# Two small matrix products of a fused transformer kernel as quadrant tiles, with a new interleaving of its first stretch

## The chip, the cores and the metric

The kernel runs as one program on one core of a Trainium2 chip. The metric is the device time of one launch in microseconds. The engines are TensorE (PE, with its weight loads PEld), VectorE (DVE), ScalarE (ACT), GpSimd (POOL) and SyncE (SP); DMAs are issued by SP, ACT and POOL and moved by the core's 16 DMA engines.

## What is computed

A block of six layers over 2048 tokens of width 256 (32 batches of 64), in float32:

```python
x = x + _L0_xattn_ref(_layernorm(x), ctx_768, mask, ...)   # 8 heads of 64 over 256 context rows
x = x + _L0_attn_ref(_layernorm(x), ...)                   # 16 heads of 16, keys and values through a latent
x = x + _L0_ffn_ref(...)                                   # ternary weights
x = x + _L1_xattn_ref(...)                                 # 16 heads of 16
x = x + _L1_attn_ref(...)                                  # gated, squared relu
x = x + _L1_ffn_ref(...)                                   # 160 experts, top 8
```

The change lies in the second layer:

```python
q = (x @ wq.T).reshape(b, s, NH, HD).transpose(0, 2, 1, 3)
k = (x @ wk_a.T @ wk_b.T).reshape(b, s, NH, HD).transpose(0, 2, 1, 3)
v = (x @ wv_a.T @ wv_b.T).reshape(b, s, NH, HD).transpose(0, 2, 1, 3)
```

`x @ wk_a.T` and `x @ wv_a.T` are 64 wide each (the latents); `@ wk_b.T` and `@ wv_b.T` bring them back to 256. These last two are the latent key and value products.

## The kernel before

The 2048 tokens are 16 tiles of 128 (`TILES`), two batches in a tile. The program has three stretches: `phase1` (layers one and two and the norm of the third, all tiles), `phase2` (layers three to five and the routing) and `experts` (layer six). A barrier of all engines stands behind `phase1`. The change is in `phase1`.

Each engine works through its instructions in the order in which they were written, and waits on semaphores at the instructions that need another engine's result. That order comes from `weave`: every part of a tile's work (`keys`, `queries`, `attend`, `unit` 0 to 3, `latent`, `half` 0 and 1, `project`, and so on) is a generator whose `yield` gives the due time of the piece that follows; tile i's parts start at i times a period; and `weave` always writes the piece that is due first. The due times are only an order: nothing waits for them on the chip.

What the prediction's steps touch, with the lines of the profile:

- `keys` (L1261): SP loads the context tile (L1265); for tile 1 it also fetches the weight group "o" (rope table, rotation inputs, `head` and others, L1232), for tile 2 the 31 weights of the later stretches, `loads` (L1277), each adding 16 to `s_load`. PE multiplies by the key weights: L1288 (128 rows) and L1293 (the other 64 rows).
- `keys_out` (L1296): ACT copies the four key banks out, L1302. `queries` (L1328): statistics L1254 to L1256, PE transposes L1361, `xT` L1366, product L1373, ACT copies `qT` out, L1378.
- `attend` (L1417): 16 score products of 64x64 tiles, L1429, in two groups of eight; the first needs `qT` and key copies 0 and 1, the second copies 2 and 3.
- `unit` (L1380): DVE masks and takes the maxima (L1385, L1388), ACT exponentiates (L1396), PE transposes (L1409), DVE or ACT copies out (L1415). `values` L1312, L1317; `gather` L1447 and on.
- `latent` (L1478): PE transposes (L1494), latent product L1508 and queries L1512, ACT copies `lat` (L1516); then the key product L1520 and the value product L1525, both from the 64-row halves of `lat`; DVE copies `qTB` (L1531) and `vx` (L1544), ACT `kx` (L1536). `half` (L1548): score products L1558 (its second group needs `vx`), maxima, exponentials L1572, transposes L1582. `project` (L1589): L1607, L1612, L1627.
- `clearing` (L1644): ACT issues 16 DMAs of 1768 KB that clear the routing table (L1649). `rotate` (L1651): DVE turns the query and key weights by the rope table in three pieces of six operations (L1661 to L1667); the first waits for group "o". `prepare` (L1670): DVE and PE wait until all 31 `loads` have landed (`s_load`), then DVE reduces and scales a few of them (L1674 to L1703).

```python
period = 34.25
parts = [(467.91, keys_values(0, banks_free)), (110.00, clearing()), (41.72, rotate()), (37.04, prepare())]
```

Of the kernel before, what the change touches and what calls it, by code (L numbers as in the profile page):

```python
# [15 lines left out]
P = 128  # L16
# [24 lines left out]
NEG = -3.4028234663852886e38  # L41

# [117 lines left out]
def weave(parts):  # L160

    due = []
    for start, part in parts:
        due.append([start + next(part), len(due), start, part])
    while due:
        due.sort()
        first = due[0]
        at = next(first[3], None)
        if at is None:
            due.remove(first)  # L170
        else:
            first[0] = max(first[0], first[2] + at)


def later_keys(nc, a, G, D, bank, cT, kT, vv, weights, s_ctx):

    pe, act, sp = nc.tensor, nc.scalar, nc.sync
    wka, wkb, wva, wvb, bkd = weights

    def keys_values(i, banks_free=None):  # L180
        z = i % 2
        yield 5.96
        G.wait(sp, "v3", i - 2)
        sp.dma_start(cT[z][:, :, :], a["ctx2"][i]).then_inc(s_ctx[z], 16)
        yield 144.95
# [6 lines left out]
        yield 157.65  # L192
# [3 lines left out]
        for m in range(2):  # L196
            yield (168.53, 169.89)[m]
# [3 lines left out]
        yield 168.10  # L201
        for m in range(2):
            D.wait(pe, f"e{6 + m}", i - 1)
        for t in range(2):
            yield (173.60, 175.54)[t]
            cols = slice(t * DIM, (t + 1) * DIM)
            for m in range(2):
                q = 2 * m + t
# [4 lines left out]
        for m in range(2):  # L213
            yield (180.74, 182.84)[m]
# [7 lines left out]
def phase2(nc, a, turns, keys_values, routes, rings, sem, bank, X, XN, ident, small, dchain, pool_waits, resident, kT, vv, qs, qb, bg2, sc):  # L222
# [5 lines left out]
    with ph:  # L228
# [104 lines left out]
        def stage_c(i):  # L333
            z = i % 2
            yield 131.54
# [5 lines left out]
            yield 135.57  # L341
# [3 lines left out]
            yield 142.54  # L345
# [4 lines left out]
            yield 143.99  # L350
# [6 lines left out]
            yield 145.18  # L357
            C.wait(pool, "var", i)
            C.done(i, "pool", power(stC), "rstd")
            yield 146.27  # L360
# [3 lines left out]
            yield 150.06  # L364
# [3 lines left out]
            yield 149.36  # L368
# [4 lines left out]
            yield 155.21  # L373
# [3 lines left out]
            yield 155.72  # L377
# [7 lines left out]
            yield 160.29  # L385
# [8 lines left out]
        def scores(i, m):  # L394
            z = i % 2
            yield (155.05, 168.93)[m]
# [13 lines left out]
        def softmax(i, u):  # L410
            m, hp, bk = u // 4, u % 4, bank[4 + u % 2]
            yield (161.78, 161.28, 161.07, 163.97, 168.75, 169.00, 192.86, 170.02)[u]
# [3 lines left out]
            yield (163.54, 163.20, 162.31, 166.80, 175.29, 179.64, 199.05, 188.63)[u]  # L416
# [7 lines left out]
            yield (187.67, 162.00, 194.66, 169.27, 200.15, 189.54, 205.24, 196.98)[u]  # L424
# [11 lines left out]
            yield (196.45, 168.22, 195.16, 182.33, 203.51, 197.43, 207.47, 203.11)[u]  # L436
# [5 lines left out]
        def mix(i):  # L442
            z = i % 2
            for m in range(2):
                yield (167.68, 198.02)[m]
# [3 lines left out]
                yield (182.00, 201.83)[m]  # L449
# [7 lines left out]
            yield 204.98  # L457
# [6 lines left out]
            yield 210.31  # L464
            D.wait(pe, "pT6e", i)
            D.wait(pe, "pT7e", i)
# [10 lines left out]
            yield 210.32  # L477
# [3 lines left out]
            yield 210.82  # L481
# [9 lines left out]
            yield 210.82  # L491
# [6 lines left out]
        def stage_e(j):  # L498
            z = j % 2
            yield 196.97  # L500
# [7 lines left out]
            yield 201.92  # L508
            E.wait(pool, "vara", j)
            E.done(j, "pool", power(stE), "rstda")  # L510
            yield 212.05
# [3 lines left out]
            yield 222.30  # L515
# [4 lines left out]
            yield 226.39  # L520
            E.wait(pool, "x5", j - 1)
            E.done(j, "pool", pool.tensor_tensor(xbE[:, :], x4[:, :], bout[:, :], ALU.add), "xbE")
            yield 223.12
# [5 lines left out]
            yield 225.83  # L529
# [3 lines left out]
            yield 233.13  # L533
# [5 lines left out]
            yield 233.39  # L539
# [3 lines left out]
            yield 235.02  # L543
# [4 lines left out]
            yield 234.13  # L548
# [6 lines left out]
            yield 234.92  # L555
# [3 lines left out]
            yield 241.28  # L559
# [6 lines left out]
            yield 235.46  # L566
# [3 lines left out]
            yield 240.77  # L570
# [3 lines left out]
            yield 240.93  # L574
# [3 lines left out]
            yield 241.90  # L578
# [7 lines left out]
            yield 243.21  # L586
# [8 lines left out]
            yield 245.33  # L595
# [5 lines left out]
            yield 244.64  # L601
# [7 lines left out]
            yield 247.42  # L609
# [4 lines left out]
            yield 249.36  # L614
# [5 lines left out]
            yield 249.89  # L620
            E.wait(pool, "varf", j)
            E.done(j, "pool", power(stE), "rstdf")
            yield 252.75
# [8 lines left out]
            yield 253.88  # L632
# [14 lines left out]
        def stage_f(j):  # L647
            z = j % 2
            yield 238.29
# [5 lines left out]
            yield 236.18  # L655
# [3 lines left out]
            yield 239.29  # L659
# [4 lines left out]
            yield 241.15  # L664
# [3 lines left out]
            yield 244.18  # L668
# [3 lines left out]
            yield 244.18  # L672
# [7 lines left out]
            yield 246.99  # L680
# [3 lines left out]
            yield 248.84  # L684
# [6 lines left out]
            yield 248.84  # L691
            R.wait(pe, "before", j)
            R.done(j, "pe", pe.matmul(after, ones[:, 0, :], before[z][:, :], start=True, stop=True), "rank")
            yield 270.19
# [12 lines left out]
            yield 272.07  # L707
# [7 lines left out]
            yield 279.76  # L715
# [3 lines left out]
            for k in range(TOPK):  # L719
                yield (280.87, 280.87, 281.74, 285.93, 290.87, 307.02, 329.57, 324.60)[k]  # L720
# [6 lines left out]
        def count_pages(j):  # L727
            yield 273.00
# [10 lines left out]
        def order_pages():  # L739
# [3 lines left out]
            yield -30.00  # L743
            D.wait(sp, "norm", TILES - 1)
            sp.dma_start(numbers, bc(a["c_pages"], 0, P)).then_inc(s_ids, 16)
            yield 1.00
# [3 lines left out]
            yield 1.50  # L750
# [5 lines left out]
            yield 3.50  # L756
# [95 lines left out]
        for i in range(TILES):  # L852
            parts += [(i * period + 24.00, scores(i, m)) for m in range(2)] + [(i * period + 24.00, softmax(i, u)) for u in range(8)]
            if i:
                parts.append((i * period, keys_values(i)))
# [981 lines left out]
```

## Time and profile before

| | us |
|---|---|
| median of 3 runs | 1413.94 |
| lowest and highest | 1410.7, 1417.48 |
| span of the profiled execution, first to last instruction | 1412.0 |
| own time of the profiled execution | not listed apart from its span |
| of it: `phase1` with its weights' loading | about 486 |
| `phase2` | about 540 |
| `experts` | the rest |

The profile's rows give for an instruction or a run of equal ones the start, the time, the engine, the line, the operation, what it writes and reads, its shape and how often. A float32 matmul leaves two records (x4 is two matmuls), a transpose one. Times that stand behind "PE" are modelled at their end: the distance from one start to the next is the safer measure. Matmuls run on parts of the array at once where their rows and columns of it differ; such a group's records overlap.

### The profile page before, as it was taken

How to read it: one execution, taken by the hardware profiler on the slowest of the kernel's cores; microseconds unless marked ns; L12 is line 12 of the kernel's file. 1: busy time of each engine (PE TensorE's matmuls, PEld its weight loads, DVE VectorE, ACT ScalarE, POOL GpSimd, SP SyncE). 2: the span in 40 equal slices, each digit the busy share in tenths (PEclk: the TensorE clock that was granted, in tenths of full speed). 3: DMA queues.
4: the chain of work that ended last, by engine and by line, in shares of the span. 5: the costliest groups of instructions: out<-in, count | busy, mean ns of one | idle time of the engine just before them, and what ended most of it. 6: DMA issues, size and time to landing. Idle time of an engine off the chain costs nothing. (4 is left out here: it accounts for less than half of the span.)

```text
span 1412.0 us, 33973 instructions
## 1 busy us (share of the span) xinstructions
PE 1268.7 (90%) x11501; PEld 894.2 (63%) x11501; DVE 975.7 (69%) x2708; ACT 574.7 (41%) x1675; POOL 545.0 (39%) x721
## 2 busy tenths in 40 slices
PE   7999999999999679989998998997757999999946
PEld 4666666666666456666666666665536777777725
DVE  3766666666666446888788888877645777777737
ACT  3445444544454156656556566654200111111140
POOL 1110111011100102556555655565524777767730
PEclk9999999999999789999999999999778999999968
DMA  8532322423230000111121111111369889999758
GB/s 257 159 119 81 114 74 68 133 69 118 68 103 33 30 16 20 52 52 59 64 70 52 55 59 52 55 49 50 107 186 262 239 258 278 266 290 267 227 206 363
DMA packets 122571, 179.39 MB, mean 127 GB/s; under 512 B 23029, under 2 KB 90260, under 8 KB 120480
## 3 DMA queue, kind: packets, MB, share of 16 engines
q1 hardware_dynamic: 50992, 84.84, 19.5%
q10 hardware_dynamic: 55280, 57.73, 13.4%
q0 software_dynamic: 16128, 34.67, 7.0%
q8 instruction: 93, 1.52, 0.5%
q14 instruction: 78, 0.64, 0.2%
HBM read 184.59 MB, written 78.25 MB: 186 GB/s over the span
## 5 line engine op out<-in xcount | busy, mean ns | idle before, releaser
L1002 POOL DMA_INDIRECT y_d<-y,xg x208 | 205.2, 986 | 119.0 <-DVE y L998 70.6
L722 POOL DMA_INDIRECT xs_d<-xw,slot_id x128 | 133.2, 1041 | 36.8 <-issue 31.1
L971 ACT ACTIVATE ex<-bank 128x512 f32<-128x512 f32 x52 | 31.1, 598 | 280.4 <-PE bank L966 171.3
L421 ACT ACTIVATE ex<-bank,nmC 128x256 f32<-128x256 f32 x256 | 119.9, 491 | 8.7 <-DVE nmC L415 8.1
L955 DVE COPY ex<-bank 128x512 f32<-128x512 f32 x104 | 67.3, 687 | 72.8 <-PE bank L951 43.5
L434 PE MATMUL bank<-ident,ex 128*128 128x128 f32 x512 | 80.8, 282 | 27.5 <-DVE pTC L440 13.4
L434 PEld LDWEIGHTS bank<-ident,ex 128*128 128x128 f32 x512 | 57.2, 142 | 74.4 <-issue 31.0
L415 DVE TENSOR_REDUCE nmC<-bank 128x2 f32<-128x512 f32 x128 | 82.0, 684 | 7.8 <-PE bank L406 7.8
L998 DVE COPY y<-bank 128x512 f32<-128x512 f32 x104 | 71.8, 691 | 19.6 <-PE bank L992 15.6
L951 PE MATMUL bank<-ident,xg 128*128 128x128 f32 x416 | 59.2, 287 | 19.6 <-DMA xg<-xs_d 19.6
L1598 POOL COPY recxB<-recB 128x128 f32<-128x128 f32 x32 | 8.4, 292 | 177.1 <-DVE recB L1593 177.1
L1259 POOL TENSOR_TENSOR stB<-stB,small 128x1 f32<-128x1 f32 x32 | 20.2, 633 | 140.7 <-DVE stB L1256 140.7
L1396 ACT ACTIVATE sm<-sm,nm 128x256 f32<-128x256 f32 x128 | 63.5, 500 | 15.8 <-DVE nm L1388 15.8
L1288 PE MATMUL bank<-cT,wk0a 128*128 128x512 f32 x128 | 62.6, 613 | 7.8 <-DMA wk0b<-in_wk0b 7.8
L951 PEld LDWEIGHTS bank<-ident,xg 128*128 128x128 f32 x416 | 46.6, 145 | 29.1 <-DMA xg<-xs_d 21.1
L1312 PE MATMUL bank<-wv0a,cT 128*128 128x512 f32 x128 | 60.3, 593 | 0.1
L406 PE MATMUL bank<-kTC,qxC 32*128 32x256 f32 x512 | 50.0, 426 | 10.5 <-ACT ex L421 10.1
L421 ACT ACTIVATION_READ_ACCUMULATOR ex<-bank,nmC 128x1 f32 x256 | 56.8, 222 | 0.0
L217 ACT COPY vvC<-bank 128x512 f32<-128x512 f32 x32 | 17.2, 589 | 92.2 <-PE bank L212 92.2
L440 ACT COPY pTC<-bank 128x512 f32<-128x512 f32 x80 | 48.1, 640 | 9.3 <-PE bank L434 9.3
L1388 DVE CUSTOM_DVE_ANT_0 sm<-bank,mb 128x256 f32<-128x256 f32 x128 | 49.3, 423 | 3.3
L1259 POOL TENSOR_TENSOR stA<-stA,small 128x1 f32<-128x1 f32 x16 | 8.8, 549 | 110.2 <-DVE stA L1256 110.2
(386 smaller groups left out, 3345.7 us busy)
## 6 DMA issues: line engine op xcount, KB each, us to landing
xs_d<-zeros ACTq DMA_DIRECT2D x16, 1768.0 KB, 7.2
pTC<-in_wexp SPq DMA_DIRECT2D x104, 256.0 KB
xg<-xs_d ACTq DMA_DIRECT2D x312, 68.0 KB
cT<-in_ctx SPq DMA_DIRECT2D x32, 512.0 KB, 3.7
wh<-in_wexp SPq DMA_DIRECT2D x52, 256.0 KB
cT<-in_wexp SPq DMA_DIRECT2D x52, 256.0 KB
kTC<-in_wexp SPq DMA_DIRECT2D x52, 256.0 KB
vvC<-in_wexp SPq DMA_DIRECT2D x52, 256.0 KB
```

What stands on the lines that cost most here:

```text
L406: last = pe.matmul(bank[hp][:, 256 * b:256 * b + 256], qx[z][rows, m, b, :, :].rearrange("p h t -> p (h t)"), kT[z][rows, m, 256 * b:256 * ...
L415: D.done(i, "dve", dve.tensor_reduce(nm[:, u, :], bank[hp][:, :].rearrange("p (b n) -> p b n", b=2), AX.X, ALU.max, negate=True), f"m{u}")
L421: last = act.activation(ex[:, u, 256 * b:256 * b + 256], bank[hp][:, 256 * b:256 * b + 256], ACT.Exp, bias=nm[:, u, b:b + 1], accum_out=su ...
L434: last = pe.transpose(bk[:, q * P:(q + 1) * P], ex[:, u, q * P:(q + 1) * P], ident[:, :])
L722: pool.indirect_dma_start(out=xs_d, out_offset=bass.IndirectOffsetOnAxis(ap=slot_id[z][:, k:k + 1], axis=0), in_=xw[z][:, k, :], in_offset ...
L951: last = pe.transpose(bk[:, (2 * c + g) * P:(2 * c + g + 1) * P], xg[:, d % FETCHED, g, c * P:(c + 1) * P], ident[:, :])
L955: T.done("dve", dve.tensor_copy(xgT[d % 4], bk[:, :]))
L998: D.done("dve", dve.tensor_copy(y[:, n, :, :].rearrange("p g n -> p (g n)"), bk[:, :]))
L1002: pool.indirect_dma_start(out=y_d, out_offset=bass.IndirectOffsetOnAxis(ap=who, axis=0), in_=y[:, n, g, :], in_offset=None, bounds_check=l ...
L1288: pe.matmul(bank[m][:, :], wka[:, m * P:(m + 1) * P], cT[z][:, 0, :], start=True, stop=False)
L1312: pe.matmul(bank[q][:, :], cT[z][:, 0, q * P:(q + 1) * P], wva[:, :], start=True, stop=False)
L1396: last = act.activation(sm[:, j, n, :], sm[:, j, n, :], ACT.Exp, bias=nm[:, h:h + 1], scale=-1.0, accum_out=sums[:, h:h + 1])
```

## The change

In `latent`, the key product was two matmuls with 64 rows and all 128 columns of the array, and the value product four matmuls with 64 rows and 64 columns. Now both are four matmuls of 64x64, written alternately so that four in a row stand on the four quadrants of the array: keys use the upper 64 rows (bank 6), values the lower 64 rows (bank 7).

The due times move out of the `yield`s into two tables, `ORDER1` for the first stretch and `ORDER2` for the second, and `weave` reads them there. Those of the first stretch are new; those of the second give the order that stood before.

```diff
-            for m in range(2):
-                last = pe.matmul(bank[6][:, 256 + m * P:256 + (m + 1) * P], wlb[0:64, m * P:(m + 1) * P], lat[0:64, :], start=True, stop=True)
-            B.done(i, "pe", last, "qk")
             wv = wlb[64:128, :].rearrange("p (u h d) -> p h u d", u=8, h=2)
-            for b in range(2):
+            for n in range(2):
                 for h in range(2):
-                    last = pe.matmul(bank[7][64 * h:64 * h + 64, b * P:(b + 1) * P].rearrange("p (u d) -> p u d", u=8), lat[64:128, 64 * b:64 * b + 64],
-                                     wv[:, h, :, :], start=True, stop=True)
-            B.done(i, "pe", last, "v")
+                    rows = slice(64 * h, 64 * h + 64)
+                    k = pe.matmul(bank[6][rows, 256 + n * P:256 + (n + 1) * P], wlb[0:64, n * P + 64 * h:n * P + 64 * h + 64], lat[0:64, :],
+                                  start=True, stop=True)
+                    v = pe.matmul(bank[7][rows, n * P:(n + 1) * P].rearrange("p (u d) -> p u d", u=8), lat[64:128, 64 * n:64 * n + 64],
+                                  wv[:, h, :, :], start=True, stop=True)
+            B.done(i, "pe", k, "qk")
+            B.done(i, "pe", v, "v")
...
+ORDER1 = {
...
+    "rotate": (57.98, 57.99, 78.72, 87.35),
...
+    "clearing": (68.64, 78.43, 84.19, 101.45, 101.74, 137.72, 172.55, 247.38, 263.78, 306.38, 347.82, 357.61, 381.21, 393.88, 448.56, 540.95),
...
+    "prepare": (103.18, 122.18, 124.48, 127.36, 128.80, 129.66),
```

**TensorE, one tile in the steady part of the first stretch.** Before, from the key product L1293 to the second value product:

```order
L1293 MATMUL bank<-cT,wk0b 128x512 x4
L1494 MATMUL bank<-ident,xnB 128x128 x2
L1429 MATMUL bank<-kTA,qTA 64x256 x16
L1508 MATMUL bank<-xTB,wla 128x128 x2
L1512 MATMUL bank<-xTB,wqs 128x128 x4
L1312 MATMUL bank<-wv0a,cT 128x512 x2
L1409 MATMUL bank<-ident,sm 128x128 x4
L1520 MATMUL bank<-lat,wlb 128x128 x2
L1525 MATMUL bank<-wlb,lat 64x128 x4
L1409 MATMUL bank<-ident,sm 128x128 x4
```

The same place in the changed kernel (its lines are 49 or 50 further on: L1342 is L1293, L1478 is L1429):

```order
L1342 MATMUL bank<-cT,wk0b 128x512 x4
L1543 MATMUL bank<-ident,xnB 128x128 x2
L1478 MATMUL bank<-kTA,qTA 64x256 x8
L1557 MATMUL bank<-xTB,wla 128x128 x2
L1561 MATMUL bank<-xTB,wqs 128x128 x4
L1478 MATMUL bank<-kTA,qTA 64x256 x8
L1572 MATMUL bank<-lat,wlb 64x128
L1574 MATMUL bank<-wlb,lat 64x128
...
L1361 MATMUL bank<-wv0a,cT 128x512 x2
L1458 MATMUL bank<-ident,sm 128x128 x4
```

The 16 score products are split, the latent products of queries stand between their halves, and the eight new products (four pairs, one shown) follow the second half at once.

**VectorE at the start of the program.** Before, tile 0's first unit (L1385) follows the first mask; in the changed kernel the first piece of `rotate` (L1711 to L1717), with its wait for group "o", and the statistics of tiles 1 and 2 stand ahead of it:

```order
L1403 TENSOR_SCALAR mb<-mk 128x256 [waits s_weights_m]
L1396 TENSOR_SCALAR xnA<-X,stA 128x256 [waits Q_pe,Q_pool]
L1711 TENSOR_TENSOR t<-pTB,rope 128x128 [waits s_weights_o]
L1712 TENSOR_TENSOR t<-pTB,rope 128x128
L1713 TENSOR_TENSOR wqs<-t 128x128 [waits dve_chain]
L1715 TENSOR_TENSOR t<-pTB,rope 128x128
L1716 TENSOR_TENSOR t<-pTB,rope 128x128
L1717 TENSOR_TENSOR wqs<-t 128x128 [waits dve_chain]
L1303 BN_STATS stA<-X 128x6 [waits dve_chain]
L1304 BN_AGGR stA<-stA 128x2 [waits dve_chain]
L1305 TENSOR_SCALAR stA<-stA 128x1 [waits dve_chain]
L1434 MEMSET idle 1x1 [waits A_pe]
```

In tile 1, the wait of `prepare` for all loads was behind `oTB` (L1622), near the tile's end; it now stands behind `qTB`, ahead of the copies `pTA` and `vx` that TensorE needs in the middle of the tile:

```order
L1581 COPY qTB<-bank 128x256 [waits B_pe]
L1724 TENSOR_REDUCE sc<-wf 128x1 [waits s_load]
L1725 TENSOR_SCALAR bqd<-bqd 128x2
L1726 TENSOR_SCALAR bqk<-bqk 128x1
L1727 TENSOR_SCALAR qs<-head 128x2
L1728 TENSOR_SCALAR bg<-bg 128x4
L1730 TENSOR_SCALAR both<-c_ones,bvd 128x128 x2
L1464 COPY pTA<-bank 128x512 [waits A_pe]
L1594 COPY vx<-bank 64x16x16 [waits B_pe]
```

**ScalarE in tiles 0 and 1**, the changed kernel. Before, the first clearing DMA stood in tile 1 behind all its exponentials, the next ones about a tile apart, and `qTA` stood ahead of all four `kTA`:

```order
L1445 ACTIVATE sm,sums<-sm,nm 128x256 x4
L1699 DMA xs_d<-zeros 1664x1x272
...
L1375 COPY vvA<-bank 128x512 x2
L1699 DMA xs_d<-zeros 1664x1x272
L1464 COPY pTA<-bank 128x512
L1699 DMA xs_d<-zeros 1664x1x272
...
L1351 COPY kTA<-bank 128x512
L1427 COPY qTA<-bank 128x512
L1351 COPY kTA<-bank 128x512 x2
...
L1445 ACTIVATE sm,sums<-sm,nm 128x256 x4
L1699 DMA xs_d<-zeros 1664x1x272 x2
```

Five of the 16 clearing DMAs are now issued in tiles 0 and 1, and in every tile one key copy stands ahead of `qTA`, and the first of them waits for L1293's first products. SP's order is the same in both. Behind the last tile's L191 (the first product of `keys_values`), its second one, L195, now follows at once; it stood behind L1558 before.

## Rows read from the trace of the kernel before

**Rows 1.** Head of the page.

```profile
span 1412.0 us, 33973 instructions
```

**Rows 2.** Busy time by stretch: stretch, its length, each engine's busy time (instructions), clock, DMA share, GB/s.

```profile
100.00:440.00 340.00, 339.73 (x3359) 226.54 (x3351) 214.66 (x707) 164.07 (x438) 36.34 (x72) 1.00 0.29 94
440.00:486.00 46.00, 38.05 (x331) 25.25 (x329) 24.09 (x67) 15.69 (x38) 3.33 (x9) 0.85 0.01 1
```

**Rows 3.** Timeline of PE, one steady tile: start, us, engine, line, operation, tiles, shape, records.

```profile
202.64 1.88 PE L1288 MATMUL bank<-cT,wk0a 128*128 128x512 f32 x4
204.36 1.03 PE L1627 MATMUL bank<-wos,oTB 128*128 128x256 f32 x4
...
208.82 1.99 PE L1293 MATMUL bank<-cT,wk0b 64*128 64x512 f32 x8
...
211.20 2.07 PE L1429 MATMUL bank<-kTA,qTA 64*64 64x256 f32 x32
213.20 0.71 PE L1508 MATMUL bank<-xTB,wla 128*128 128x128 f32 x4
...
216.90 0.71 PE L1520 MATMUL bank<-lat,wlb 64*128 64x128 f32 x4
...
218.12 0.66 PE L1409 MATMUL bank<-ident,sm 128*128 128x128 f32 x4
...
229.19 0.65 PE L1607 MATMUL bank<-pTB,vx 128*32 128x64 f32 x32
...
230.83 1.88 PE L1288 MATMUL bank<-cT,wk0a 128*128 128x512 f32 x4
```

**Rows 4.** Timeline of ACT, the same tile.

```profile
208.93 0.59 ACT L1378 COPY qTA<-bank 128x512 f32<-128x512 f32 x1 [5.23 <-PE bank L1373]
209.98 2.05 ACT L1302 COPY kTA<-bank 128x512 f32<-128x512 f32 x4 [0.47 <-PE bank L1293]
```

**Rows 5.** Timeline of DVE, tiles 0 and 1.

```profile
19.44 0.06 DVE L1385 MEMSET idle<- 1x1 f32 x1 [6.45 <-PE bank L1429]
...
32.34 0.28 DVE L1661 TENSOR_TENSOR t<-pTB,rope 128x128 f32<-128x128 f32 x1
...
47.40 0.42 DVE L1531 COPY qTB<-bank 128x256 f32<-128x256 f32 x1 [1.15 <-PE bank L1520]
...
60.82 0.68 DVE L1674 TENSOR_REDUCE sc<-wf 128x1 f32<-128x512 f32 x1
```

**Rows 6.** SP's last issues of group "o" and of `loads`, and the first of tile 2.

```profile
16.71 0.43 SPq L1232 DMA_DIRECT2D head<-in_c_head  x1
...
26.99 0.33 SPq L1265 DMA_DIRECT2D cT<-in_ctx  x1
...
47.89 0.43 SPq L1277 DMA_DIRECT2D half<-in_c_half  x1
```

**Rows 7.** Time from issue to landing, of `head`, then of `half`.

```profile
DMA to landing us min/median/max: 5.3/5.3/5.3
DMA to landing us min/median/max: 2.4/2.4/2.4
```

**Rows 8.** DMA queues: packets, MB, share of 16 engines; SP's from 27 to 50, then ACT's from 72 to 80 (one clearing).

```profile
q1 hardware_dynamic: 6032, 5.14, 80.8%
...
q10 hardware_dynamic: 1680, 1.81, 65.6%
```

**Rows 9.** Timeline of PE: tile 1's first L1558, then the last tile's end.

```profile
50.18 0.68 PE L1558 MATMUL bank<-kx,qTB 32*64 32x128 f32 x16
...
462.30 0.44 PE L1494 MATMUL bank<-ident,xnB 128*128 128x128 f32 x2 [1.53 <-DVE xnB L1489]
...
465.94 1.09 PE L1520 MATMUL bank<-lat,wlb 64*128 64x128 f32 x4
466.96 0.65 PE L1525 MATMUL bank<-wlb,lat 64*64 64x128 f32 x8
...
471.89 2.08 PE L195 MATMUL bank<-cT,wkb 64*128 64x512 f32 x4
```

**Rows 10.** Busy time by stretch, at the last tile's end.

```profile
464.00:466.00 2.00, 2.00 (x11) 1.77 (x10) 0.00 (x0) 0.27 (x1) 0.00 (x0) 0.50 0.00 0
```

More of the change, by code:

```diff
@@ L157, in wait, with weave @@
             eng.wait_ge(self.sem[e], i * self.per[e] + k)
-def weave(parts):
+def weave(parts, order):
     due = []
-    for start, part in parts:
-        due.append([start + next(part), len(due), start, part])
+    for start, name, part in parts:
+        next(part)
+        due.append([start + order[name][0], len(due), start, part, 0, order[name]])
     while due:
@@ L167, in weave @@
         first = due[0]
-        at = next(first[3], None)
-        if at is None:
+        if next(first[3], due) is due:
             due.remove(first)
         else:
-            first[0] = max(first[0], first[2] + at)
+            first[4] += 1
+            first[0] = max(first[0], first[2] + first[5][first[4]])
 def later_keys(nc, a, G, D, bank, cT, kT, vv, weights, s_ctx):
@@ L463, in mix @@
             D.done(i, "pe", last, "recT")
-            yield 210.31
-            D.wait(pe, "pT6e", i)
-            D.wait(pe, "pT7e", i)
+            yield
+            D.wait(pe, ("pT2e", "pT4e", "pT6e"), i)
+            D.wait(pe, ("pT0e", "pT1e", "pT3e", "pT5e", "pT7e"), i)
             for m in range(2):
@@ L820, in common_up @@
             for n in range(TILES // 2):
-                yield 2.20 * n if n < 7 else 28.00
+                yield
                 V.wait(pe, "act", n)
@@ L832, in common_down @@
             for n in range(TILES // 2):
-                yield 2.20 * n if n < 3 else (21.80, 22.30, 25.30, 25.80, 26.30)[n - 3]
+                yield
                 if n == 0:
@@ L1329, in queries @@
             z = i % 2
-            yield 39.27
+            yield
             if i == 0:
@@ L1479, in latent @@
             z = i % 2
-            yield 70.60
+            yield
             A.wait(dve, "x1", i)
             mean_var(B, i, stB, x1[z][:, :], "var")
-            yield 74.92
+            yield
             B.wait(pool, "var", i)
             B.done(i, "pool", power(stB), "rstd")
-            yield 74.99
+            yield
             B.wait(dve, "rstd", i)
@@ L1708, in banks_free @@
                 K.wait(pe, f"v{q}e", TILES - 1)
-        period = 34.25
-        parts = [(467.91, keys_values(0, banks_free)), (110.00, clearing()), (41.72, rotate()), (37.04, prepare())]
+        parts = [(0.0, "keys_values", keys_values(0, banks_free))] + [(0.0, p.__name__, p()) for p in (clearing, rotate, prepare)]
         for i in range(TILES):
-            at = i * period
-            parts += [(at, keys(i)), (at, keys_out(i)), (at, values(i)), (at, values_out(i)), (at, queries(i)), (at, attend(i)), (at, gather(i)), (at + 25.40, latent(i)), (at + 25.40, project(i))]
-            parts += [(at, unit(i, j)) for j in range(4)] + [(at + 25.70, half(i, f)) for f in range(2)]
-        weave(parts)
+            at = i * PERIOD1
+            parts += [(at, p.__name__, p(i)) for p in (keys, keys_out, values, values_out, queries, attend, gather, latent, project)]
+            parts += [(at, f"unit{j}", unit(i, j)) for j in range(4)] + [(at, f"half{f}", half(i, f)) for f in range(2)]
+        weave(parts, ORDER1)
         B.wait(dve, "xn3", TILES - 1)
```

328 lines of the change are left out of this document (185 added, 143 removed).

## The prediction

> **What bounds the kernel.** I read the head of the page, then the busy times by stretch, then the first stretch's timelines. The profiled execution spans 1412.0 us [rows 1], 1.9 under the median of 1413.94; I sum against the span and add 1.9 at the end. Phase2 and the experts keep their orders and their instructions, so I give them no change. In the first stretch TensorE is busy 339.73 of 340 us with a clock of 1.00, while VectorE has 125 us and ScalarE 176 to spare and the DMAs stand at 0.29 [rows 2]. So what happens there between 100 and 440 us is worth what it does to TensorE's chain, and nothing else. At two ends it is different. At the start, weights still arrive: VectorE waited 6.45 us for the first scores, and began at 19.44 [rows 5]. In 440 to 486 the granted clock is 0.85 [rows 2], and at 464 to 466 it is 0.50, the lower of its two levels, after TensorE had idled 1.53 us for `xnB` [rows 9, 10].
>
> **Start, first wait.** The first piece of `rotate` now stands ahead of tile 0's first unit, with its wait for group "o". SP's order is unchanged: `head`, the last of the group, is issued at 16.71 and lands 5.3 us later [rows 6, 7], at 22.0. Six operations of 0.28 us in steps of about 0.24 follow, then the three statistics (some 0.7), so the unit starts at 24.4 in place of 19.44. Behind VectorE stand ScalarE's exponentials and TensorE's first value product, which waits for a bank that the unit frees. TensorE had no spare work there, so this is **+4.9**, at least 4 (an earlier landing of the rope table alone) and at most 5. The rotation was cheap where it stood before: 32.34 lay in a gap of VectorE while TensorE worked [rows 5].
>
> **Start, second wait.** `prepare` waits for all 31 loads. It was reached at 60.82 and found them there: the last, `half`, was issued at 47.89 and landed 2.4 later [rows 6, 7]. Now it is reached behind `qTB`: 47.40 [rows 5] plus 0.42 plus the shift of 4.9 is about 52.5. Queued behind it on VectorE are `pTA` and `vx`. TensorE runs dry soon after: the value products of the self attention wait on `vx`, and TensorE carries the same wait itself ahead of its 64-row value products.
> When do the loads land? SP issues them behind tile 2's context, 26.99 before [rows 6] and 31.9 now, and the first bytes move some 2 us later, 33.9. Without more traffic than before, everything is 4.9 later: 47.89 + 2.4 + 4.9 = 55.2. But ScalarE now issues five clearings in tiles 0 and 1, where there was none before 48. One clearing takes 8 us at a share of 65.6%, which is 5.25 us of all 16 DMA engines; the loads' stretch of 23 us ran at 80.8%, 18.6 us of them [rows 8], so they have little room. Four of the clearings stand ahead of or beside the loads. With two of them counted in full the loads land at 33.9 + 18.6 + 2 x 5.25 = 63.0. With four, whose 6720 packets alternate with the loads' 6032 [rows 8], 33.9 + 18.6 + the loads' number of clearing packets, 3.6 clearings or 18.9, is 71.4. I take 66, between the two, since the first clearing is issued some 5 us before the loads and is mostly through. TensorE's stall is the landing, plus 1.3 for `prepare`, 0.6 and 0.9 for `pTA` and `vx`, against its own need of `vx` at 50.18 + 4.9 + 0.3 = 55.4 [rows 9]: landing minus 52.6, so **+13.5**. The bounds are 2.7 (55.2) and 18.9 (71.4). Of this, the rule of the Trainium skill, page "DMA: Bandwidth & Descriptors", section "Queues, rings and completion order", would choose: each DMA engine goes round between the queues that have work for it, a packet from each in turn, which favours 71.4 and a time near 1433. No row shows two such queues at once, so I stay between.
> After an idle time of over 10 us the clock may stand at its lower level for a while, as it did after 1.53 us at 462 [rows 9, 10]: **+1**, from 0 to 3.
>
> **Steady tile, 14 times.** The key and value products take 218.12 - 216.90 = 1.22 us [rows 3]. The new eight leave 16 records. L1429 shows what quadrants give: 32 records of 256 columns in 2.00 us [rows 3]; at 0.84 ns a column-step with four at once it would be 32 x 256 / 4 x 0.84 = 1.72, and 0.28 remains for entry. The new ones: 16 records of 128 columns, four at once, are 512 steps, 0.43 us. That saves 0.79. L1429 is cut in two, one more entry, +0.28. Third, one key copy now stands ahead of `qTA`. Before, ScalarE did `qTA` at 208.93 in time it had, idled 0.47, and copied keys from 209.98 every 0.51 us, so the second key copy ended at 211.0 and TensorE began the scores at 211.20 [rows 3, 4]. Now the first key copy is bound to 209.98 as before, `qTA` follows, and the second ends at 211.5, a stall of 0.3. The sum is -0.79 + 0.28 + 0.29 = -0.22 a tile, **-3.1**. The bounds: no stall and no entry, -0.79 or -11.1; a second entry of 0.28 and the full 0.5 of the copy, +0.27 or +3.8.
> Against this stands a rule of the Trainium skill, page "TensorE: Matmul & The Clock Gate", section "Wait — 56ns, not 53.3ns?": with hardware decode off the sequencer needs about 62 ns per matmul. By it 16 records could not go under 1.0 us, the tile would lose 0.35 and the sum be about 8 us higher. The row speaks against it: L1607 runs 32 records in 0.65 us [rows 3], 20 ns each, so the sum goes without it.
> The clearings themselves, and the other steps moved on VectorE and ScalarE in the steady tiles, I cost at nothing: TensorE's 339.73 of 340 covers them; were that cover gone, a clearing costs ScalarE's queue one issue.
>
> **Last tile.** The key and value products run at half clock there, 465.94 and 466.96 for 1.09 and 0.65 [rows 9]; the new ones take about 0.9 in place of 1.7. L195, at 471.89 before, moves into the idle 1.53 us ahead of L1494 [rows 9]. At least -1.2. If TensorE then never idles, the clock may stay at its upper level, and most of 0.15 x 46 = 6.9 us comes back [rows 2]; I allow 6. Other waits of that tile remain (no next tile's work fills them), so I take **-2.5**.
>
> Sum: 4.9 + 13.5 + 1.0 - 3.1 - 2.5 = +13.8, 1425.8 on the span, 1427.7 against the median.
>
> **Rivals.**
> A: the clearings don't delay the loads. The DMAs' rates in 27 to 50 left a fifth idle [rows 8], and a clearing's packets are no smaller (1.81 MB in 1680), so the loads may keep their pace. Then 4.9 + 2.7 + 0 - 3.1 - 2.5 = +2.0, about 1416.
> B: faster. TensorE is the bound, and gets its saving in full: the key copy comes in time, L1429's cut costs nothing, and the tail keeps its clock, -11.1 - 6. For it: ScalarE has 176 of 340 us idle [rows 2], and in the new order the first key copy may find its product sooner, since it doesn't wait behind `qTA`. Against it: the slack at the scores was 0.2 us. It decides only with the loads landing near 55.2, since then the start costs 7.6: that gives -9.5, 1404.4. The point from which it beats "no change" is a saving over 0.36 us a tile, with the tail's 2.5.
> C: the quadrants don't overlap, and the change does not do what it says. Eight matmuls one after the other, 16 records of 0.107 us, are 1.71 against 1.22; that with the rest is +1.06 a tile in place of -0.22, +17.9 on my sum, 1446. L1429's and L1607's rows speak against it [rows 3], only the mix of two products speaks for it.
>
> **Numbers.** The forecast's mechanism (VectorE waits for group "o" and then for loads that come late) 0.56; A 0.22; B 0.18; C 0.04. A measurement of this kernel can tell 0.5%, 7 us, from no change. In the forecast's case the low end with loads at 58 is 1419.6, still "same" by a little; I count 0.04 of its 0.56 there and C as slower, so slower is 0.56, same 0.25 (A, and that end), faster 0.19. The range takes in A and B and the forecast's upper bound: 71.4 in place of 66 adds 5.4, and two more of clock and the steady tiles' error 5 or so: 1404 to 1440, with C and the far ends outside. Alone, the likeliest case has 1419 to 1440.
>
> **What would show it.** In the profile after: VectorE's first unit starts near 24.4 and what ends the wait before the first `rotate` row is a DMA of group "o"; in tile 1, an idle of over 10 us on VectorE ahead of the reduction of `wf` (L1724), ended by one of the loads' DMAs, with clearings under way in the DMA queues, and TensorE idle beside it. In a steady tile the eight products take about 0.45 us, TensorE idles about 0.3 ahead of L1478 for `kTA`, and the period falls from 28.19 (202.64 to 230.83 [rows 3]) to about 27.97. At the end L195 stands ahead of L1543. It would be wrong if the wait before L1724 were under 5 us, if the period fell under 27.6 or rose, or if phase2's span changed.

## The result and the profile after

The changed kernel takes 1441.93 us (median of 4 runs, 1441.19 to 1446.46) against 1415.71 before (median of 4): a ratio of 1.0207 with a 95% interval of 1.0175 to 1.0239. It is slower by 25 to 34 us where 13.8 was forecast, and 1.9 us above the range's end of 1440.

The profiled execution spans 1440.1 us. Three of TensorE's starts on the two traces split the difference: `recx`'s transposes of tile 0 (L1612 before, L1662 after), the same of tile 15, and the first instruction of phase2 (L299, L348).

| | before | after | later by |
|---|---|---|---|
| tile 0's L1612 / L1662 | 59.53 | 86.26 | 26.7 |
| tile 15's | 477.64 | 499.87 | 22.2 |
| L299 / L348, phase2 | 485.74 | 508.27 | 22.5 |
| end of the span | 1412.0 | 1440.1 | 28.1 |

All of the loss in the first stretch arises before 86 us; the steady tiles and the last one give 4 us back. The last 5.6 us arise in phase2 and the experts, whose orders are unchanged. From the first expert transpose to the end took 359.7 us before and 363.5 after; in six more profiles of kernels that differ only in the first stretch (e5, e6, e8 to e11 below) it took 356.6 to 361.5 us. Over the whole rest, from phase2's start to the end, these six and e7 took 922.2 to 932.2 us; the kernel before took 926.3, the changed one 931.8. So I read these 5.6 us as the scatter of later stretches that one execution shows.

**The start.** VectorE's timeline of the changed kernel, with tile 0's first unit and tile 1's `prepare` (columns as in [rows 5]: start, time, and in brackets the idle before it and who ended it):

```profile
21.85 0.29 DVE L1711 TENSOR_TENSOR t<-pTB,rope 128x128 f32<-128x128 f32 x1 [4.81 <-DMA head<-in_c_head]
...
24.21 0.06 DVE L1434 MEMSET idle<- 1x1 f32 x1
...
71.23 0.69 DVE L1724 TENSOR_REDUCE sc<-wf 128x1 f32<-128x512 f32 x1 [17.61 <-DMA half<-in_c_half]
```

Both waits stand where they were forecast: the unit starts at 24.21 (24.4 was said), and VectorE then idles 17.61 us for `half`. TensorE beside it:

```profile
20.16 2.08 PE L1478 MATMUL bank<-kTA,qTA 64*64 64x256 f32 x32 [0.88 <-ACT kTA L1351]
25.25 3.63 PE L1361 MATMUL bank<-wv0a,cT 128*128 128x512 f32 x4 [3.02 <-DVE nm L1437]
...
46.89 0.44 PE L1543 MATMUL bank<-ident,xnB 128*128 128x128 f32 x2
...
58.31 0.65 PE L1608 MATMUL bank<-kx,qTB 32*64 32x128 f32 x8 [1.88 <-ACT kx L1586]
74.00 1.12 PE L1608 MATMUL bank<-kx,qTB 32*64 32x128 f32 x8 [15.03 <-DVE vx L1594]
75.04 3.79 PE L1366 MATMUL bank<-wv0b,cT 64*128 64x512 f32 x8
```

L1361 starts 4.8 us later than L1312 did (20.46), but then takes 3.63 in place of 1.96; the `xnB` transposes of tile 0's second layer, L1543, start at 46.89, and the same (L1494) started at 40.49 before. So 6.4 us are lost up to there, and the other 20.3 of the 26.7 between there and L1662. L1366 takes 3.79 in place of 1.99. That is the lower clock: the granted clock was 0.55 from 25.00 to 28.68, near 0.50, the lower of its two levels, and 0.50 from 74 to 80. The busy times by stretch (last numbers: granted clock, DMA share, GB/s):

```profile
20.00:30.00 10.00, 6.82 (x42) 3.37 (x43) 5.98 (x30) 4.05 (x15) 0.55 (x1) 0.83 0.85 276
60.00:70.00 10.00, 0.00 (x0) 0.00 (x0) 0.00 (x0) 0.69 (x4) 0.00 (x0) 0.50 1.09 375
74.00:80.00 6.00, 6.00 (x33) 2.81 (x34) 2.71 (x8) 1.70 (x3) 0.00 (x0) 0.50 0.05 7
100.00:440.00 340.00, 334.37 (x3420) 222.46 (x3421) 219.97 (x713) 166.05 (x440) 35.18 (x71) 1.00 0.25 80
```

From 60 to 70 us the DMA engines are full (1.09) and TensorE does nothing; after it, TensorE runs at 0.50. The last line answers [rows 2]: 334.37 of 340 us busy where it was 339.73.

ScalarE's and SP's issues in that time (the number behind the start is how long the issue took):

```profile
50.76 0.54 ACTq L1699 DMA_DIRECT2D xs_d<-zeros  x1
51.34 6.04 ACTq L1699 DMA_DIRECT2D xs_d<-zeros  x1
57.42 0.84 ACT L1586 ACTIVATE kx<-bank,head 128x256 f32<-128x256 f32 x2 [5.43 <-issue]
```

```profile
33.85 0.44 SPq L1326 DMA_DIRECT2D wf<-in_wf  x1
...
62.23 0.59 SPq L1326 DMA_DIRECT2D half<-in_c_half  x1
```

The issue of the fifth clearing, directly behind the fourth, held ScalarE for 6.04 us, and `kx` behind it. TensorE idled 1.88 us for `kx` at 58.31, but that lies inside the wait that follows: the second half of L1608 needs `vx` and starts at 74.00 in any case. The queues from the first load's issue to the last one's landing, 33.85 to 71.23:

```profile
q10 hardware_dynamic: 6704, 7.23, 53.8%
q1 hardware_dynamic: 6032, 5.14, 47.1%
```

Nearly as many clearing packets (q10) as packets of loads (q1) were moved, 37.4 us for what took 22.9 before (27.36 to 50.3). They alternated through all of that time, not only in the sum: 1628 beside 1401 up to 45 us, then 1186 beside 957 (to 51), 946 beside 936 (to 58), 883 beside 886 (to 62) and 2061 beside 1852.

**A steady tile.** TensorE, from the scores to the next value product, answering [rows 3]:

```profile
208.98 0.44 PE L1543 MATMUL bank<-ident,xnB 128*128 128x128 f32 x2 [0.20 <-DVE xnB L1538]
209.66 1.09 PE L1478 MATMUL bank<-kTA,qTA 64*64 64x256 f32 x16 [0.24 <-ACT kTA L1351]
210.68 0.71 PE L1557 MATMUL bank<-xTB,wla 128*128 128x128 f32 x4
...
213.13 0.27 PE L1572 MATMUL bank<-lat,wlb 64*64 64x128 f32 x1
213.14 0.27 PE L1574 MATMUL bank<-wlb,lat 64*64 64x128 f32 x1
213.14 0.27 PE L1572 MATMUL bank<-lat,wlb 64*64 64x128 f32 x1
213.15 0.27 PE L1574 MATMUL bank<-wlb,lat 64*64 64x128 f32 x1
213.24 0.27 PE L1572 MATMUL bank<-lat,wlb 64*64 64x128 f32 x1
...
213.68 1.99 PE L1361 MATMUL bank<-wv0a,cT 128*128 128x512 f32 x4
```

Four records start within 0.02 us, then four more 0.11 later: the quadrants do overlap, and 16 records take 213.68 - 213.13 = 0.55 us in place of 1.22. But two idles, 0.20 for `xnB` and 0.24 for a key copy, stand ahead of the scores, and the period is 28.08 (199.67 to 227.75 for L1662) against 28.19.

### The profile page after: what moved, and what is told of

Same layout as the page of the kernel before. It is cut to its first block and busy times, and to the rows that moved or that the text cites. A ratio compares the mean times of both kernels' runs of the same rounds, so it can differ in the third digit from the quotient of the medians.

```text
span 1440.1 us, 34103 instructions
## 1 busy us (share of the span) xinstructions
PE 1267.1 (88%) x11565; PEld 892.4 (62%) x11565; DVE 980.6 (68%) x2708; ACT 575.3 (40%) x1675; POOL 544.6 (38%) x721
## 5 line engine op out<-in xcount | busy, mean ns | idle before, releaser
L483 PE MATMUL bank<-ident,ex 128*128 128x128 f32 x512 | 82.0, 285 | 26.8 <-DVE pTC L489 13.6
L1351 ACT COPY kTA<-bank 128x512 f32<-128x512 f32 x64 | 37.1, 613 | 76.1 <-PE bank L1342 76.1
L1361 PE MATMUL bank<-wv0a,cT 128*128 128x512 f32 x128 | 63.5, 620 | 3.0 <-DVE nm L1437 3.0
L1000 PEld LDWEIGHTS bank<-ident,xg 128*128 128x128 f32 x416 | 46.7, 146 | 28.7 <-DMA xg<-xs_d 20.3
L489 ACT COPY pTC<-bank 128x512 f32<-128x512 f32 x80 | 47.8, 635 | 10.3 <-PE bank L483 10.3
```

The source lines that it names most:

```text
L483: last = pe.transpose(bk[:, q * P:(q + 1) * P], ex[:, u, q * P:(q + 1) * P], ident[:, :])
L1000: last = pe.transpose(bk[:, (2 * c + g) * P:(2 * c + g + 1) * P], xg[:, d % FETCHED, g, c * P:(c + 1) * P], ident[:, :])
L1361: pe.matmul(bank[q][:, :], cT[z][:, 0, q * P:(q + 1) * P], wva[:, :], start=True, stop=False)
```

## The experiments

The runs of e1 to e4 were on a chip on which every kernel takes some 180 us more in the experts (before: 1592.5); its first stretch runs as on the others. So the ratios are to the kernel before on the same chip. The kernel before has no trace from that chip, and the stretch is compared with its trace from another: the steady tiles agree (28.08 us in e2 as in the changed kernel), the start only roughly. Tile 0 up to L1543 has the same order in the changed kernel and in e2, e3, e9 and e10, and L1543 starts at 46.89, 48.33, 48.16, 46.59 and 45.90: TensorE's first scores begin at 19.41 to 22.16, so the idle behind them is 1.73 to 3.98 us, and L1361 runs at the lower clock behind it for none, part or all of its matmuls. So single starts differ by up to 2.5 us without any edit, and from L1543 to L1662 is the better measure of the second wait. All are in the table at the end of this section.

**e1: the new products alone**, in the old order: the `+` lines of the diff's first part in the kernel before, nothing else.

```diff
-                last = pe.matmul(bank[6][:, 256 + m * P:256 + (m + 1) * P], wlb[0:64, m * P:(m + 1) * P], lat[0:64, :], start=True, stop=True)
...
+                    k = pe.matmul(bank[6][rows, 256 + n * P:256 + (n + 1) * P], wlb[0:64, n * P + 64 * h:n * P + 64 * h + 64], lat[0:64, :],
+                                  start=True, stop=True)
```

> The kernel before with only the key and value products replaced, at their old place in the order. If the products save what the changed kernel's trace shows (the group takes 0.55 us in place of 1.22) and TensorE's chain is the bound of a tile, the period falls from 28.19 to about 27.52 and the kernel is 10 us faster (ratio 0.993). Rival: what is saved turns into a wait for ScalarE's kx or VectorE's vx, the period stays above 28.0 and the time within 3 us of before.

Ratio 0.9937 (0.9918 to 0.9956), about 10 us faster, as expected. The group takes 0.60 us here, the period is 27.57, and TensorE is as full as before (busy times by stretch of e1):

```profile
100.00:440.00 340.00, 339.72 (x3466) 224.23 (x3465) 217.87 (x713) 168.43 (x449) 36.51 (x72) 1.00 0.27 92
```

0.62 us a tile reach the period in full. The products were the good half of the change.

**e2: the wait for the loads back behind `oTB`.**

```diff
-    "prepare": (103.18, 122.18, ...
+    "prepare": (119.31, 122.18, ...
```

> The changed kernel with the first piece of prepare (the wait for all loads) back behind oTB of tile 1, everything else as changed. If the wait's place is the cost, the 15 us idle ahead of L1608 in tile 1 goes; the loads still land near 71, by then VectorE stands near 69, so TensorE waits at most 3 us, and the time falls by 15 to 17 us against the changed kernel, to 8 to 12 above before. Rival: the late loads cost wherever the wait stands (TensorE itself waits ahead of L1366 by the same piece of prepare); then under 6 us comes back.

**e3: the clearings back at their old due times.**

```diff
-    "clearing": (68.64, 78.43, 84.19, 101.45, 101.74, 137.72, ...
+    "clearing": (110.00, 140.00, 170.00, 200.00, 230.00, 260.00, ...
```

> The changed kernel with the 16 clearing DMAs issued at the due times of before, the wait for the loads staying early. If the clearings delayed the loads, half lands near 62 in place of 71.2 (62 is its old 50.3 plus 6.5 of later start plus some) and 8 to 12 us come back. Rival: the loads are late because SP issues them late, behind tile 2's context; then half lands after 66 and under 5 us comes back.

Ratios 1.0038 (1.0016 to 1.0060) and 1.0049 (1.0023 to 1.0076). The first stretch ends at 493.45 and 493.49 in place of 508.27: each of the two, alone, takes away 14.8 us, about what was expected of e2 (15 to 17) and more than of e3 (8 to 12). In e3 the loads, with the wait still early, are nearly there (VectorE's timeline of e3):

```profile
57.64 0.69 DVE L1724 TENSOR_REDUCE sc<-wf 128x1 f32<-128x512 f32 x1 [2.75 <-DMA half<-in_c_half]
```

They landed 13.6 us earlier than in the changed kernel, though SP issued the first of them 1.3 later (35.12). I had expected 62; they are as fast as before, 22.5 us from the first issue. SP's own issues, 28.4 us from the first to the last in the changed kernel, take 19.5 (35.12 to 54.64): SP was slower while the clearings moved, not because of what stands ahead of the loads. So the rival of e3 falls, and that of e2, under 6 us, too. What is left of the wait in e3 is an idle of 2.12 us for `vx` (TensorE's timeline of e3):

```profile
60.41 0.65 PE L1608 MATMUL bank<-kx,qTB 32*64 32x128 f32 x8 [2.12 <-DVE vx L1594]
60.99 3.08 PE L1366 MATMUL bank<-wv0b,cT 64*128 64x512 f32 x8
```

In e2 what is left of the early clearings is the held `kx`, here a cost of its own (TensorE's timeline of e2):

```profile
60.23 0.78 PE L1608 MATMUL bank<-kx,qTB 32*64 32x128 f32 x16 [2.35 <-ACT kx L1586]
60.94 2.74 PE L1366 MATMUL bank<-wv0b,cT 64*128 64x512 f32 x8
```

**e9: both of these back together.**

> The changed kernel with both prepare and the clearings back, rotate and the key copy as changed. Each alone brought the first stretch's end some 15 us forward (508.27 to 493.45 and 493.49). If they are two halves of one wait, both together bring only what was left of it, 2 to 3 us more (end near 491). Rival: they are two costs, and both together bring near 30 us (end near 479).

Ratio 1.0030 (1.0008 to 1.0053). The stretch ends at 487.74, 20.5 us earlier than in the changed kernel. Two separate costs would have given 29.6, one shared wait and nothing else 14.8. Part of the difference stands ahead of the wait: L1543 starts 1.6 to 1.7 us earlier here than in e2 and e3. From L1543 to L1662 it is 39.37 us in the changed kernel, 22.92 in e2, 23.34 in e3, and 19.04 both here and in the kernel before. So with both edits nothing is left of the second wait, which cost 20.3 us; either edit alone removes 16.0 to 16.5 of it, and 3.9 to 4.3 go only with both. In e2 these are the 2.35 us idle for `kx` and the lower clock behind it (L1366 takes 2.74 in place of 1.99), in e3 the 2.12 us of idle for `vx` and the clock (3.08). That is still more than the 2 to 3 expected.

**e10: two of the five clearings early.**

```diff
+    "clearing": (68.64, 78.43, 170.00, 200.00, 230.00, 260.00, ...
```

> The changed kernel with only the first two of the five early clearings left early (68.64 and 78.43), the rest at the old due times. The first is mostly through when the loads start, so one competes with them. If the two queues share the DMA engines packet for packet, the last load lands one clearing's 5.3 us later than without clearings (57.6 plus 5 to 6, near 63), and the wait ahead of L1724 is 8 us. Rival: one clearing is absorbed in the 19% that the loads left idle, and the landing stays within 1.5 us of 57.6.

VectorE's timeline of e10:

```profile
59.67 0.69 DVE L1724 TENSOR_REDUCE sc<-wf 128x1 f32<-128x512 f32 x1 [7.04 <-DMA half<-in_c_half]
```

The loads took 26.8 us from their first issue (32.87) to 59.67, 4.3 more than in e3. In that time 1743 clearing packets were moved, one clearing's number. The price of one is 4.3 us, from one profile each: not absorbed, and a little under the 5 to 6 expected. (With all five clearings early, the same time is 36.8 us in e7 and 38.8 in e6, whose edits lie elsewhere, so some 2 us of it are scatter.) The absolute time of landing, where 63 was said, is earlier mainly because SP began 2.3 us earlier than in e3.

**e5: the first piece of `rotate` back behind `oA`.**

```diff
-    "rotate": (57.98, 57.99, 78.72, 87.35),
+    "rotate": (57.98, 87.33, 87.34, 87.35),
```

> The changed kernel with the first piece of rotate back behind tile 0's oA. Tile 0's first unit then waits for TensorE's scores alone, as before, and starts within 1.5 us of them; TensorE's 3 to 4 us idle ahead of L1361 goes. If that wait costs in full, the end of the first stretch comes 4 to 5 us earlier. Rival: the wait for the loads in tile 1 swallows it, because what SP issues later also lands later or not; then tile 1's end stays within 1 us if the loads' landing doesn't move, and moves with it if it does.

VectorE's timeline of e5:

```profile
21.41 0.06 DVE L1434 MEMSET idle<- 1x1 f32 x1 [3.50 <-PE bank L1478]
...
69.79 0.69 DVE L1724 TENSOR_REDUCE sc<-wf 128x1 f32<-128x512 f32 x1 [20.68 <-DMA half<-in_c_half]
```

Tile 0's unit starts 2.8 us earlier, tile 1's scores 4.5 earlier (43.32 in place of 47.84), but VectorE waits 20.68 in place of 17.61 us, and the stretch ends only 3.15 earlier, at 505.12 (ratio 1.0138, 1.0095 to 1.0181). The loads are issued 4.5 us earlier and land only 1.4 earlier: the clearings come earlier too, and 7040 of their packets are moved in that time in place of 6704. So most of what the first wait cost was hidden by the second. (At tile 0's L1662 it is 2.3 us, near the scatter above. The ratio is lower by more than the stretch says, but the two intervals overlap, and the rest of this profile, 922.2 us, is the shortest of all.)

**e11: tile 0's first transposes back** between the first key products, where they stood before; the change had put them behind all four, which I had not costed.

```diff
+    "queries0": (-7.91, 11.37, 19.72, 41.01, 46.60, 52.53, 55.40, 56.84),
...
+    parts += [(at, "queries0" if p is queries and i == 0 else p.__name__, p(i)) for p in (...)]
```

> The changed kernel with tile 0's two xnA transposes between the first key products again. ScalarE's table load then runs beside L1337's second half, and the first scores (L1478) start near 18.3 in place of 20.16. If the wait for group o ends last there, nothing comes of it: the first rotate operation stays at 21.8 to 22.2 and the end of tile 0 moves under 0.5 us. Rival: TensorE's own chain ends last there, and the 1.9 us come back.

TensorE's timeline of e11:

```profile
17.91 2.08 PE L1479 MATMUL bank<-kTA,qTA 64*64 64x256 f32 x32 [0.88 <-ACT kTA L1352]
25.77 3.75 PE L1362 MATMUL bank<-wv0a,cT 128*128 128x512 f32 x4 [5.79 <-DVE nm L1438]
```

The scores start 2.25 us earlier, and the idle behind them grows from 3.02 to 5.79: nothing is gained, the stretch ends at 510.70, 2.4 later. Of these, 1.6 stand at L1543's counterpart (48.52): the first rotate operation came at 22.37 (21.85 in the changed kernel), and L1362 ran at the lower clock for longer. e2 and e3 show as much without this edit (48.33 and 48.16), so they need not come from it. The wait for group "o" ends last there. Where that wait is gone, the step does cost: e5, with the transposes as changed, reaches L1543 at 42.37, 1.9 us after the kernel before (40.49), and e4, with them back, at 39.97.

**e6: `qTA` ahead of all four key copies again.**

```diff
-    "keys_out": (55.12, 57.42, ...
+    "keys_out": (57.00, 57.42, ...
```

> The changed kernel with qTA ahead of all four key copies again. If the key copy ahead of qTA is the stall ahead of L1478, the period of a steady tile falls from 28.08 to 27.8 (0.24 idle and what follows), and the start stays as in the changed kernel. Rival: the stall comes from elsewhere (L1342's end, xnB); the period stays within 0.1 of 28.08.

The period is 27.78 (199.56 to 227.34), 0.30 less, and the idle ahead of L1478 is gone; the one ahead of `xnB`'s transposes stays (TensorE's timeline of e6):

```profile
208.88 0.44 PE L1543 MATMUL bank<-ident,xnB 128*128 128x128 f32 x2 [0.21 <-DVE xnB L1538]
```

**e7: the old products in the new order.**

> The changed kernel's order with the old two products (six matmuls) in their new place. If the new products save 0.6 us a tile also here, the period rises from 28.08 to 28.7 and the kernel is 8 to 10 us slower than the changed one. Rival: the idle ahead of the next matmuls shrinks by the same amount, and the period stays under 28.3.

The period is 28.87, 0.79 over the changed kernel's, and the ratio 1.0229 (1.0183 to 1.0275). Its stretch ends 8.7 us later than the changed kernel's, as expected; the two ratios don't tell them apart, as their intervals overlap. Against 28.19 before, the new order alone costs 0.68 us a steady tile; the products give it back. Of the 0.79, the group itself is 0.68 (1.23 and 0.55), and the scores ahead of it take 0.11 longer from their start to the group's (1.02 and 0.91).

**e4: all five moves back**, the new products and the rest of the order as changed.

> The changed kernel with five moves undone: rotate behind oA, prepare behind oTB, clearings at the old due times, one key copy behind qTA again in all tiles, and the first transposes between the first key products. New products and the tail's order stay. If the start and the key copy are the whole loss: TensorE reaches tile 1's end within 1 us of before (L1612's like at 59.5), the period is 27.6 or less, and the kernel is 8 to 14 us faster than before. Rival: the rest of the new interleaving (split scores, xnB) costs by itself; the period stays near 28.0 and the time is within 5 us of before.

Ratio 0.9946 (0.9926 to 0.9966), tile 0's L1662 at 58.52. The period is 27.78, as in e6 and 0.21 over e1's: that is what the split scores and the late `xnB` cost in every tile, so both readings were partly right.

**e8: e1 and the tail.** L195 directly behind L191, as the change has it.

```diff
-        yield 157.65
+        yield 157.65 if i else 144.96
```

> The kernel before with the new products at the old place, and the last tile's second key product of the later stretch (L195) directly behind the first one. Against e1: the 1.53 us idle ahead of L1494 is filled, so the first stretch ends 1 to 1.5 us earlier still; ratio to before 0.992 to 0.993. Rival: the last tile is bound by its chain of VectorE and ScalarE, and the end doesn't move.

TensorE's timeline of e8, the last tile:

```profile
450.81 1.13 PE L195 MATMUL bank<-cT,wkb 64*128 64x512 f32 x4
452.40 0.44 PE L1494 MATMUL bank<-ident,xnB 128*128 128x128 f32 x2 [0.47 <-DVE xnB L1489]
...
460.74 1.09 PE L1583 MATMUL bank<-ident,pB 128*128 128x128 f32 x4 [0.29 <-DVE pB L1568]
462.10 1.12 PE L1583 MATMUL bank<-ident,pB 128*128 128x128 f32 x4 [0.27 <-ACT pB L1573]
```

The idle of 1.53 is 0.47, but L1494 starts no earlier (`xnB` comes when it comes), and L195 is missing as a filler ahead of L1583, where TensorE now waits. From the fifteenth L1613 (444.31 in e1, 444.89 here) to phase2 it is 27.6 us in e1 and 28.5 in e8. That is not the price of the move: e4, e5 and e10, which move L195 as well, took 27.55, 27.67 and 27.76. What differs is the mean clock granted in this time: 0.88 in e1, e4, e5 and e10, and 0.82 in e8 and the changed kernel. So the expected 1 to 1.5 us are not there, and any price of the move lies within the scatter of the clock. Ratio 0.9929 (0.9905 to 0.9952), the same as e1 within the intervals; either beats both kernels, and e1 is the simpler.

Starts on TensorE, us:

| | tile 0's L1543 | tile 0's L1662 | period | phase2 begins | ratio to before |
|---|---|---|---|---|---|
| before | 40.49 | 59.53 | 28.19 | 485.74 | 1 |
| changed | 46.89 | 86.26 | 28.08 | 508.27 | 1.0207 |
| e1 new products alone | 39.43 | 57.84 | 27.57 | 471.94 | 0.9937 |
| e2 prepare back | 48.33 | 71.25 | 28.08 | 493.45 | 1.0038 |
| e3 clearings back | 48.16 | 71.50 | 28.09 | 493.49 | 1.0049 |
| e9 both back | 46.59 | 65.63 | 28.08 | 487.74 | 1.0030 |
| e10 two clearings early | 45.90 | 74.24 | 28.08 | 495.73 | one run |
| e5 rotate back | 42.37 | 83.96 | 28.08 | 505.12 | 1.0138 |
| e11 transposes back | 48.52 | 88.56 | 28.08 | 510.70 | one run |
| e6 key copy back | 46.80 | 87.11 | 27.78 | 504.93 | one run |
| e7 old products | 45.34 | 84.17 | 28.87 | 516.95 | 1.0229 |
| e4 all five back | 39.97 | 58.52 | 27.78 | 475.40 | 0.9946 |
| e8 e1 and the tail | 40.00 | 58.41 | 27.57 | 473.41 | 0.9929 |

## Why the prediction was wrong

The mechanism was right, slower by two waits at the start that the steady tiles don't repay, and the size was half of what was measured. The term that failed is the second wait. By the terms:

- **First wait, +4.9.** The unit started at 24.21 and L1361 4.8 us late, as said. But 6.4 us were lost up to L1543: behind the 3.02 us idle the clock was the lower one, and L1361 alone lost 1.7 us by it. I had put a clock term behind the second wait only. The step on the first transposes, which I left out, cost nothing of its own while this wait stood (e11). And e5 showed that this term is not additive: without it 2.3 us come back at L1662 and 3.15 at phase2, not 6.4.
- **Second wait, +13.5, with +1 for the clock.** This is the step that failed: 20.3 was measured (26.7 - 6.4). The mis-sized part is the landing of the loads, 71.2 and not 66. From their start, 1.6 us later than I had it, I allowed 34.1 us and they took 37.7 (without clearings I had said 23.3, and e3 took 22.9). TensorE's own need of `vx` came at 56.7 (58.31 without the 1.88 for `kx`, plus 0.3) and not at 55.4, which takes 1.3 back, and it started again at 74.00, 2.8 after the landing, as said: a wait of 17.3. Then the clock: the window of 74 to 80 ran wholly at 0.50, and from 74.00 to 80.95 it took 6.95 us for what took 3.76 before, 3.2 us lost where 1 was said.
- **A cost that no term had**: the fifth clearing's issue held ScalarE 6.04 us, with `kx` behind it. In the changed kernel the longer wait for `vx` covers it; in e2, where that wait is gone, it shows as 2.35 us of idle. The prediction said that a moved step's DMAs cost ScalarE "one issue"; it did not ask what an issue costs directly behind another, with loads still moving.
- **The rule of the Trainium skill** that I weighed there, page "DMA: Bandwidth & Descriptors", section "Queues, rings and completion order" (each DMA engine goes round between its queues), came out nearer than my own choice. It gave 71.4, and 73.0 with the later start; 71.2 was measured, beside 6704 and 6032 packets of the two queues. That the two queues alternate nearly packet for packet this case's trace bears out. A clearing cost the loads 4.3 us in e10, and 3.7 in the changed kernel (14.9 over e3's 22.5, for four clearings' packets), where its own time on the 16 engines is 5.25 by [rows 8].
- **Steady tile, -0.22.** It was -0.11. The products alone are worth 0.62 of the period (e1), where 0.79 was said; the group takes 0.55 and not 0.43. The split cost no 0.28: from the scores to the new products it is 3.47 us without the idle, and the same rows took 3.45 before; with the old products behind it (e7) it is 3.58. The key copy's stall was 0.24 (0.29 said) and 0.30 of the period (e6). Missing was the rest of the new order, 0.21 a tile by e1 against e4; in it is an idle of 0.20 for `xnB`, whose copy comes later on VectorE. -0.62, +0.30 and +0.21 make the -0.11.
- The rule of the Trainium skill, page "TensorE: Matmul & The Clock Gate", section "Wait — 56ns, not 53.3ns?" (about 62 ns for a matmul), which I set aside on the row of L1607, did not bind: 16 records in 0.55 us are 34 ns each. The rule is for hardware decode off, and no run here shows which way the decode was.
- **Last tile, -2.5.** It was -2.5, but not for the reasons given, so the match is partly luck. Without L195's move the gain was 3.3 (e1); with the move and the old products it was 2.7 (e7: 28.3 us against 31.0, and 28.5 with the new ones at the same granted clock of 0.82), so the products show no gain there. What they share is the clock: L1512 took 1.92 us before and 1.06 in all twelve other traces, in e1 behind the same idle of 1.53 us. So the idle that I named was not enough to bring the lower clock, and why only the kernel before had it there stays open. I had also read both products as running at half clock [rows 9]; only L1520 did, as L1525's 0.65 us is what it takes in a steady tile.
- Of the rivals, A (the clearings don't delay the loads) is refuted by e3 and e10, C (no overlap) by the trace. B's mechanism, that TensorE takes the products' saving in full, is what e1 shows: -0.62 a tile. In the changed kernel it did not hold, as the key copy did not come in time (0.24 us of idle), and its condition, loads near 55, did not hold either. The chances by outcome are also off by 0.01 from the mechanisms they add up (faster 0.19 beside B's 0.18, same 0.25 beside 0.22 and 0.04).

Forecast and measured for the stretch: 4.9, 14.5, -3.1 and -2.5 make 13.8; 6.4, 20.3, -1.7 and -2.5 make 22.5. The remaining 5.6 us of the one profile lie in the later stretches, within the scatter that they show; the profiled execution is the median one, so they are what puts the median just past the range's end.

What stays open: why the first stretch's gains in e1 and e4 (13.8 and 10.3 us at phase2's start) appear as some 10 and 9 us in the ratios. The intervals (3 us to either side) allow both the full gain and a loss of 3 later on, and the start that they are compared with is from another chip.

## What to carry to other kernels

A wait for a long row of loads must be priced together with what else is issued while they move: from L1543 to L1662 the early wait without the early clearings cost 4.3 us here (e3 against e9), the clearings without the wait 3.9 (e2), and both together 20.3. Price a DMA also at its issue, because one that is issued directly behind another held the whole engine that made it, here 6 us. Compare several traces before you read a microsecond out of one: the clock alone moved the start and the last tile by 1 to 2 us between executions. And take the parts of a change apart: the products were worth 0.6 us a tile, 10 us in all, and the reordering that came with them cost more than three times that (508.27 against 471.94 at phase2's start).

## What the runs showed of the hardware

Two queues of one core shared its DMA engines almost packet for packet (6704 against 6032 over 37 us, 946 against 936 from 51 to 58). The issue of a clearing took 0.54 to 0.68 us for the first of a pair and 3.1 to 7.5 us for the one directly behind it, twice each in the changed kernel, e2, e5, e6, e7 and e11, with clearings and loads on the way; no run shows the reason. And an idle of 3.0 us on TensorE was followed by a stretch at the lower clock (L1361 3.63 us in place of 1.96), one of 1.73 us at the same place in e10 was not (1.96), and one of 1.53 us in the last tile was in the kernel before (L1508 1.11 us) and was not in e1 (0.71).
